# The third of V's products behind both score steps, in a two-layer attention kernel on one core

## What is computed

```python
def _attn(xq, xc, Wq, Wk, Wv, Wo, bo):
    q = (xq @ Wq).reshape(B, N, HEADS, D_HEAD)
    k = (xc @ Wk).reshape(B, S, HEADS, D_HEAD)
    v = (xc @ Wv).reshape(B, S, HEADS, D_HEAD)
    scores = jnp.einsum('bnhd,bshd->bhns', q, k) * scale
    attn = jax.nn.softmax(scores, axis=-1)
    out = jnp.einsum('bhns,bshd->bnhd', attn, v).reshape(B, N, HEADS * D_HEAD)
    return out @ Wo + bo

x = _attn(_ln(x, g1, b1), _ln(x, g1, b1), Wq1, Wk1, Wv1, Wo1, bo1) + x
x = _attn(_ln(x, g2, b2), context, Wq2, Wk2, Wv2, Wo2, bo2) + x
x = _geglu_ff(_ln(x, g3, b3), Wp, bp, Wf, bf) + x
```

## Time and profile before

| | |
|---|---|
| time, median of 3 runs | 451.03 us (450.54 to 451.25) |
| the profiled execution | 450.97 us, of which 449.3 us are its span |
| TensorE busy | 434.4 us, 97% of the span |
| VectorE, ScalarE, GpSimd busy | 352.9, 318.8 and 201.8 us |
| from group to group in SELF and CROSS | about 18.2 to 18.4 us, some 19.4 |

### The profile page before, as it was taken

The page is one execution under the profiler, slowest core; times in us unless marked ns, Lnnn a source line. Parts: engine busy times, 40 slices in busy tenths (PEclk is TensorE's granted clock), DMA queues, the critical chain, the costliest instruction groups (busy, mean ns, idle before and its releaser), DMA issues.

```text
span 449.3 us, 17107 instructions
## 1 busy us (share of the span) xinstructions
PE 434.4 (97%) x7513; PEld 399.4 (89%) x7513; DVE 352.9 (79%) x649; ACT 318.8 (71%) x587; POOL 201.8 (45%) x226
## 2 busy tenths in 40 slices
PE   8999999999999999999999999999999999999897
PEld 7979999898999999989989899889999777778797
DVE  4888889688797887978978789896784788898471
ACT  5686676777778768787677776876546576777763
POOL 1883332555345634555352533523342232152782
PEclk9999999999999999999999999999999999999999
DMA  7202021110200000000000000000000000000011
GB/s 230 58 4 85 3 85 28 53 48 4 63 4 4 10 3 11 12 3 10 12 2 12 3 10 13 3 3 1 2 1 19 10 12 19 4 1 4 13 36 47
DMA packets 14623, 10.61 MB, mean 24 GB/s; under 512 B 5188, under 2 KB 13592, under 8 KB 14552
## 3 DMA queue, kind: packets, MB, share of 16 engines
q1 hardware_dynamic: 14120, 9.48, 7.3%
q10 hardware_dynamic: 432, 0.07, 0.1%
HBM read 8.50 MB, written 1.05 MB: 21 GB/s over the span
## 4 chain that ended last, share of the span: by engine, by line
PE 88%; DVE 6%; ACT 2%; issue 2%; POOL 1%; DMA 1%; POOLq 0%
PE stage L683 12%; PE stage L684 11%; PE stage L685 11%; PE scp L865 8%; PE scp L788 7%; PE scp L837 6%; PE scp L944 6%; PE out0p L885 4%; PE out0p L913 4%; PE out0p L887 3%; PE out0p L886 3%; PE stage L849 3%; PE scp L805 2%; DVE pr L1417 1%; PE stage L934 1%
## 5 line engine op out<-in xcount | busy, mean ns | idle before, releaser
L1734 POOL TENSOR_TENSOR pr<-pr,rc 128x1024 f32<-128x1024 f32 (+1 forms) x32 | 59.1, 1867 | 76.5 <-DVE rc L1447 76.4
L1165 ACT ACTIVATE pr<-pr 128x1024 f32<-128x1024 f32 x48 | 50.8, 1059 | 36.7 <-DVE pr L1417 30.1
L1672 POOL TENSOR_TENSOR rstd<-veps,neghalf 128x2 f32<-128x2 f32 x32 | 22.8, 714 | 70.8 <-DVE veps L1365 70.6
L1099 ACT ACTIVATE vt<-stage 64x512 f32<-64x512 f32 x83 | 49.2, 592 | 4.8 <-PE stage L685 1.2
L1461 DVE COPY vt<-stage 64x512 f32<-64x512 f32 x45 | 31.2, 694 | 21.8 <-PE stage L685 20.9
L1412 DVE TENSOR_REDUCE mx<-scp 128x16 f32<-128x1024 f32 x32 | 39.2, 1224 | 8.9 <-PE scp L788 8.5
L1099 ACT ACTIVATE ot_h<-scp 128x512 fp32r<-128x512 f32 x64 | 33.4, 600 | 13.3 <-PE scp L865 13.3
L1467 DVE TENSOR_TENSOR ot_r<-scp,ot_h 128x512 fp32r<-128x512 f32 x64 | 40.0, 683 | 2.3 <-ACT ot_h L1099 1.0
L1099 ACT ACTIVATE k_of_heads<-stage 128x512 f32<-128x512 f32 x62 | 36.9, 598 | 5.4
L1417 DVE TENSOR_TENSOR pr<-scp,mx 128x1024 f32<-128x1024 f32 x32 | 39.2, 1224 | 1.1
L1445 DVE TENSOR_REDUCE sm<-pr 128x16 f32<-128x1024 f32 x32 | 38.0, 1188 | 0.0
(11 more groups left out here) (266 smaller groups left out, 1398.8 us busy)
## 6 DMA issues: line engine op xcount, KB each, us to landing
ctx_in<-in_ctx_dram SPq DMA_DIRECT2D x16, 96.0 KB, 2.0
masked_k<-in_L_xattn_Wo_dram SPq DMA_DIRECT2D x2, 512.0 KB, 3.8
out_dram<-rows SPq DMA_DIRECT2D x8, 128.0 KB, 1.8
rows<-in_x_dram SPq DMA_DIRECT2D x1, 768.0 KB, 9.4
pr<-in_L_xattn_Wq_dram SPq DMA_DIRECT2D x1, 512.0 KB, 4.9
pr<-in_L_xattn_Wk_dram SPq DMA_DIRECT2D x1, 512.0 KB, 6.2
pt<-in_L_xattn_Wv_dram SPq DMA_DIRECT2D x1, 512.0 KB, 7.6
rows<-in_L_xattn_Wq_dram SPq DMA_DIRECT2D x1, 512.0 KB, 5.1
```

The costliest lines, as they stand in the source:

```text
L1099: return nc.scalar.activation(dst, s, ACT.Copy)
L1165: nc.scalar.activation(pr[t][:, :], pr[t][:, :], ACT.Exp, scale=scale[s.phase]).then_inc(exped, 1)
L1734: nc.gpsimd.tensor_tensor(p, p, rc[:, t, h:, None].to_broadcast([ROWS, H - h, N]), ALU.mult)\
```

## The change

In `group` of TensorE, V's product u = 2 of `one` moves from ahead of the two score steps to a place behind them, ahead of the output projection. Products 0, 1 and 3 stay.

```diff
--- before.py
+++ after.py
@@ -1031,9 +1031,10 @@
                     turn_step(s, 1)
                     av_step(s, 0)
                     av_step(s, 1)
-                    val_step(one, range(3), s)
+                    val_step(one, range(2), s)
                     scores_step(one, 0)
                     scores_step(one, 1)
+                    val_step(one, (2,), s)
                     out_step(s, 0)
                     out_step(s, 1)
                     if two.phase == GEGLU:
```

## The result

The changed kernel takes 457.35 us (median of 4 runs, 455.52 to 458.03) where the kernel before takes 450.78 beside it (4 runs, 450.21 to 451.25): ratio 1.0145, 95% interval 1.0128 to 1.0161. It is slower by about 6.6 us. The forecast was 456.1, in a range of 454.2 to 458.9. The profiled execution took 458.03 (span 456.3), the slowest of the four; for before it was 450.97 (span 449.3). The traces so differ by 7.1, of which the medians show 6.6.

The account below looks back on a forecast made before the run. TensorE, busy 97% of the span, bounds the kernel. New waits +6.4, holes gone -1.2 and the end -0.15 make +5.05: 456.0 from the profiled 450.97, 456.1 from the median; range 454.2 to 458.9.

Parts of the forecast that it names:

- Bound and place: Whole kernel: TensorE busy 97% of the span, so only a wait it has now, or a new one, moves the time.
- the chain: Third V product, ScalarE's vt copies, x's high part, GpSimd's rest, TensorE's first projection: no slack, so the rest comes 2.22 later.
- The move of 2.22: Third V product's last matmul, later by scores' length 2.02, hole ahead of them 0.09 and own change of kind 0.11.
- The change of kind: TensorE, scores to V product: 0.11 added, about as much lost at the output projection; 0, within 0.3 in all.
- The cover: Time between rest's end and projection's weights: SELF 2.44, leaving 0.17; CROSS 1.44, so waits of 0.83 in seven groups, 0.56 in CROSS 4.
- the 6.4 of the sum: TensorE's new waits in SELF 6 to CROSS 5: 5.81 in seven groups plus 0.56 in one, +6.4 us.
- The softmax: VectorE's maximum starts 0.46 earlier, so the second exponential and third product's bank do too; the 0.10 holes go, -1.2 us.
- the sixth product's hole: SELF and CROSS query and key projections: first matmul holds its successor 0.22 instead of 0.12, awaiting a stage bank; 12 x 0.10.
- the residuals: VectorE takes them from the scores' banks; done at 51.06, second of four about 49.82; earlier scores clear both: 0.
- The end: CROSS 7's first transposes, which wait for the softmax: an allowed gain of -0.15.
- the 0.8 below: Margin under the low end for TensorE stalls without a visible wait that, as in CROSS 4, hide part of a wait.
- the allowance for other things: Upper bound: holes stay, +6.4; six SELF groups wait up to 0.2 each, +1.2; change of kind, 0.3; high end 458.9.

Follow-up runs that it names:

- The five kernels: Changed kernel with ScalarE's high parts ahead of third-product copies: 451.59 us; product between scores: 455.5; behind half the output projection: 480.18; moved only before SELF: 451.63; only elsewhere: 456.65.
- the five shifted kernels: 64 more TensorE instructions: changed kernel 463.06 us, with ScalarE's high parts first 456.39; high parts first with 3 warm-ups 453.49, 15 warm-ups 453.62; kernel before, 3 warm-ups 452.63.

## Why the prediction was right, step by step

*Bound and place.* Right. TensorE had nothing but the small holes to give, and the new waits took the time: at line 683, for ctx's rest, eight times, and never where SELF follows. The five kernels that take the lateness away, halve it, add 1.4 us to it or limit it to some groups place and remove the waits as the chain says.

*The move of 2.22.* Right in size. An undisturbed group, SELF 2 of the changed kernel, in TensorE's timeline:

```profile
67.40 0.50 PE L683 MATMUL stage<-wv_of0h,src1h 128*128 128x512 f32 x1
...
68.99 2.09 PE L788 MATMUL scp<-k_of_heads,q_of_heads 64*64 64x64 f32 x128
71.02 0.50 PE L683 MATMUL stage<-wv_of0h,src1h 128*128 128x512 f32 x1
71.35 0.40 PE L684 MATMUL stage<-wv_of0r,src1h 128*128 128x512 f32 x1
71.59 0.39 PE L685 MATMUL stage<-wv_of0h,src1r 128*128 128x512 f32 x1
71.82 0.28 PE L885 MATMUL out0p<-ot_h,wp_h 128*128 128x256 f32 x1
71.94 0.28 PE L886 MATMUL out0p<-ot_r,wp_h 128*128 128x256 f32 x1
```

From V's first product to the third's last matmul are 71.59 - 67.40 = 4.19; in SELF 1 of before it was 50.72 - 48.77 = 1.95, so 2.24. The scores start 1.59 behind V's first product (68.99 - 67.40) where it was 2.27 (51.04 - 48.77): 0.68 earlier, with 0.69 forecast. The change of kind moves as forecast from the output projection (now 0.12 at its start) to the product (71.35 - 71.02 = 0.33).

*The cover.* SELF: 0.17 forecast. The rest of SELF 1 ends at 55.55 + 0.74 = 56.29 and the weights load at 56.50, without a wait, beside the earlier trace rows. In the six groups this distance is 0.21 to 0.23; less the 0.05 from GpSimd to TensorE, 0.16 to 0.18 is left:

```profile
55.55 0.74 POOL L1700 TENSOR_TENSOR src1r<-xT,src1h 128x256 fp32r<-128x256 f32 x1 [3.74 <-ACT src1h L1100]
...
56.50 0.19 PEld L683 LDWEIGHTS stage<-src1h,wq_of0h 128*128 128x128 f32 x1
```

CROSS: 0.83 forecast, 0.83 measured in seven groups. CROSS 4 was 0.56 in the forecast and came to 0.44, since a stall of 0.39 in its output projection, more than the one of before, hid part of the wait. The two ends of the earlier trace rows in the changed kernel (weight loads):

```profile
267.15 0.19 PEld L683 LDWEIGHTS stage<-src0h,wq_of1h 128*128 128x128 f32 x1 [0.36 <-POOL ctx_src0r L1703]
...
286.23 0.19 PEld L683 LDWEIGHTS stage<-src1h,wq_of1h 128*128 128x128 f32 x1 [0.75 <-POOL ctx_src1r L1703]
```

That is 7 x 0.83 + 0.44 = 6.25 for the 6.4 of the sum.

*The softmax.* Right. VectorE's maximum in SELF 1, beside the earlier trace rows:

```profile
48.86 2.48 DVE L1468 TENSOR_TENSOR ot_r<-scp,ot_h 128x512 fp32r<-128x512 f32 x4
51.38 0.69 DVE L1462 COPY vt<-stage 64x512 f32<-64x512 f32 x1
52.10 1.23 DVE L1413 TENSOR_REDUCE mx<-scp 128x16 f32<-128x1024 f32 x1
```

The maximum starts with the copy's end, its 0.48 of idle time gone, and against the residuals it comes 0.45 earlier (52.10 - 48.86 = 3.24 for 52.27 - 48.58 = 3.69), with 0.46 forecast. So the sixth product's hole is gone, beside the earlier trace rows in TensorE's timeline, at 0.12 from start to start:

```profile
60.10 0.28 PE L685 MATMUL stage<-src1h,wk_of0r 128*128 128x256 f32 x1
60.22 0.28 PE L683 MATMUL stage<-src1h,wk_of0h 128*128 128x256 f32 x1
60.34 0.28 PE L684 MATMUL stage<-src1r,wk_of0h 128*128 128x256 f32 x1
```

All 12 have left: -1.2 as forecast. An undisturbed SELF group takes 18.07 for 18.19. The scores nowhere waited for the residuals.

*The end.* Forecast -0.15, measured -0.31: matmul by matmul, the changed kernel is 7.35 late in CROSS 6's output projection and 7.04 late behind CROSS 7's first transposes.

*What the sum lacked.* The terms as measured give 6.25 - 1.2 - 0.3 = +4.75, for the +5.05 of the sum; the profiled executions differ by 7.06. The term that was mis-sized is the stalls, which the prediction let only shorten a wait (the 0.8 below) and never add. From start to start they are 2.85 us before (at 86, 109, 235 and 258) and 4.81 after (at 33, 52, 86, 91, 111, 239, 243 and 264): +2.0. Together that is +6.75; 0.3 I can't place. The median lies 1.25 above the forecast, within the range by the allowance for other things, not by this reason; that the range held it was luck in this part. The stalls are counted in one execution of each kernel, and times of one kernel spread by 2.5 us in 4 runs (changed) and by 3.3 in 23 (before, 449.01 to 452.33), so the 2.0 is the difference of these two executions.

*Why there are more of them.* Where a stall can fall is a matter of code position, as the five shifted kernels show. That the new order has more of them is seen only by count, in one execution of each kernel: after a stall in attention times V a second one follows in the scores some 4 us later in 11 of 13 cases of the new order, as at 239.39 and 243.37, and in none of 7 of the old. The scores' 256 short instructions now stand 0.69 closer to those of attention times V, which would leave less time for the next fetch. With the product between the scores their first half is as close, and neither of two such stalls is followed by a second. No run changes this distance alone, and the cause of the second stall stays open.

## What to carry to other kernels

Where a step moves on an engine that is already full, look at what its product's consumer has queued behind it: here V's product was needed late, but two small conversions stood behind its copies on ScalarE. The cost is the shift less the cover of that second chain, separately for each kind of group (2.44 and 1.44 against 2.22). If the move is wanted anyway, turn the consumer's queue as well, which took nearly all of the loss away here.

## What the runs showed of the hardware

- TensorE can stand still in straight-line code while it waits for nothing that the profile shows: 0.2 to 1.7 us at a time from start to start and 2 to 5 us in a run of 450, ending 2.2 to 3.0 us after a 16 KB fetch on the instruction queue began. With 64 more instructions ahead the stalls stand two groups later, with 9 warm-up products fewer or more one group earlier or later.
- A product set between the two score steps costs about 0.36 us by two more changes between 64x64 and 128x512 matmuls (0.32 to 0.34 for 0.23 from start to start) and by the cut in the run of 64x64 ones (1.09 for 1.01 each half), though the list of TensorE's waits has no new one.
- Behind two of eight waits of 2.25 us TensorE's clock was granted at 0.50, 1.2 GHz, for some 3 us; behind the other six, and behind those of 0.8 in the changed kernel, it stayed at full speed.
- 64 instructions that wait for something long past took 6.9 us on TensorE ahead of its first matmul, 0.11 each.
